# Two more projections ahead of the differential attention's loop, two cross-attention units in its last heads

## The reference, cut to what matters

```python
x = x + _L0_xattn_ref(_layernorm(x), ctx_2048, ...)   # stage X0
x = x + _L0_attn_ref(_layernorm(x), ...)              # stage A0
x = x + _L0_ffn_ref(_layernorm(x), ...)               # stage F0
x = x + _L1_xattn_ref(_layernorm(x), ctx_2048, ...)   # stage X1
x = x + _L1_attn_ref(_layernorm(x), ...)              # stage M1
x = x + _L1_ffn_ref(_layernorm(x), ...)               # stage F1
```

```python
q = (x @ Wq).reshape(b, s, h, 2, dh)       # dh = 64
k = (x @ Wk).reshape(b, s, h, 2, dh)
v = (x @ Wv).reshape(b, s, h, 2 * dh)
attn1 = softmax(einsum('bhsd,bhtd->bhst', q1, k1) * scale)
attn2 = softmax(einsum('bhsd,bhtd->bhst', q2, k2) * scale)
out = einsum('bhst,bhtd->bhsd', attn1 - lam * attn2, vh)
out = (out - mu) * rsqrt(var + EPS) * gw + gb          # per head
return out.reshape(b, s, -1) @ Wo
```

## Time and profile before

| | |
|---|---|
| three runs | 672.36 us median (667.4 to 675.68) |
| profiled execution, its own time | 668.17 us |
| its span | 666.4 us |
| PE busy | 639.1 us, 96% |
| DVE, ACT, POOL busy | 63%, 41%, 9% |
| granted PE clock, mean | 0.997 |

### The profile page before, as it was taken

One profiled execution on the slowest core, in us unless ns is written; L12 is line 12 of the kernel. 1 busy time (PEld: TensorE's weight loads), 2 busy tenths in 40 slices (PEclk: granted clock), 3 DMA queues, 4 the chain that ended last, 5 costly groups with the idle time before them and its releaser, 6 DMA issues.

```text
span 666.4 us, 21584 instructions
## 1 busy us (share of the span) xinstructions
PE 639.1 (96%) x9570; PEld 429.5 (64%) x9572; DVE 421.7 (63%) x982; ACT 274.4 (41%) x502; POOL 58.8 (9%) x130
## 2 busy tenths in 40 slices
PE   9999999999978999999999999999999999999876
PEld 4666667667565566666667565776777775466754
DVE  4544568587764765555564673554888965787487
ACT  2454445445442334333433754544554454011134
POOL 1020000000000100111111003000010101000000
PEclk9999999999998999999999999999999999999999
DMA  7243112117004500011002521111167200000001
GB/s 240 64 165 67 34 33 59 40 35 223 2 3 163 187 30 9 30 33 32 2 1 82 205 63 64 34 65 34 45 174 196 66 4 1 3 3 2 3 1 33
DMA packets 42365, 42.25 MB, mean 63 GB/s; under 512 B 15904, under 2 KB 33056, under 8 KB 42016
## 3 DMA queue, kind: packets, MB, share of 16 engines
q1 hardware_dynamic: 42272, 40.86, 19.8%
HBM read 40.33 MB, written 0.52 MB: 61 GB/s over the span
## 4 chain that ended last, share of the span: by engine, by line
PE 85%; DVE 10%; issue 2%; ACT 2%; POOL 0%; DVEq 0%; ACTq 0%; POOLq 0%
PE psum L379 16%; PE psum L387 16%; PE psum L1119 7%; PE psum L454 5%; PE psum L419 4%; PE psum L429 4%; PE psum L1170 4%; PE psum L1125 4%; PE psum L1860 2%; PE psum L404 2%; PE psum L1140 2%; PE psum L1839 2%; PE psum L1820 1%; PE psum L1154 1%; DVE arena L1956 1%
## 5 line engine op out<-in xcount | busy, mean ns | idle before, releaser
L379 PE MATMUL psum<-arena 128*128 128x512 f32 x256 | 121.6, 603 | 0.0
L387 PE MATMUL psum<-arena 128*128 128x256 f32 x512 | 121.5, 384 | 0.0
L387 PEld LDWEIGHTS psum<-arena 128*128 128x128 f32 x512 | 93.9, 190 | 21.6 <-issue 9.4
L379 PEld LDWEIGHTS psum<-arena 128*128 128x128 f32 x256 | 45.1, 191 | 43.7 <-issue 41.9
L674 ACT ACTIVATE arena<-arena 128x512 f32<-128x512 f32 x64 | 47.9, 804 | 35.5 <-DVE arena L798 35.5
L668 ACT ACTIVATE arena<-psum,arena 128x512 f32<-128x512 f32 x64 | 40.2, 687 | 31.0 <-DVE arena L785 30.9
L1119 PE MATMUL psum<-y_cols,arena 128*128 128x512 f32 x112 | 52.9, 605 | 0.0
L454 PEld LDWEIGHTS psum<-arena 128*17 128x17 f32 x4096 | 38.4, 96 | 20.7 <-issue 12.9
L798 DVE TENSOR_SCALAR arena<-psum 128x512 f32<-128x512 f32 x64 | 39.7, 682 | 17.9 <-PE psum L419 17.9
L1222 ACT ACTIVATE arena<-psum 128x512 f32<-128x512 f32 x48 | 28.2, 597 | 48.2 <-PE psum L1119 30.9
L785 DVE TENSOR_REDUCE arena<-psum 128x1 f32<-128x512 f32 x64 | 39.7, 684 | 12.8 <-PE psum L404 12.5
(11 more groups left out here) (248 smaller groups left out, 932.0 us busy)
## 6 DMA issues: line engine op xcount, KB each, us to landing
arena<-in_ctxT SPq DMA_DIRECT2D x32, 512.0 KB, 3.7
arena<-in_L_attn_Wv SPq DMA_DIRECT2D x1, 2048.0 KB, 8.4
arena<-in_L_attn_Wq SPq DMA_DIRECT2D x8, 256.0 KB, 2.9
arena<-in_L_attn_Wk SPq DMA_DIRECT2D x8, 256.0 KB, 3.5
arena<-in_L_attn_Wo SPq DMA_DIRECT2D x1, 2048.0 KB, 11.6
arena<-in_L_ffn_w_gating SPq DMA_DIRECT2D x1, 2048.0 KB, 7.9
arena<-in_L_attn_wo SPq DMA_DIRECT2D x2, 1024.0 KB, 6.3
arena<-in_wq_upT SPq DMA_DIRECT2D x2, 768.0 KB, 6.7
```

The lines of the kernel that those rows point to most:

```text
L379: last = nc.tensor.matmul(bank, wkv[:, c, i * P:(i + 1) * P], x[:, c, :], start=(c == 0), stop=(c == NC - 1))
L387: last = nc.tensor.matmul(bank[:, kk * D:(kk + 1) * D], x[:, c, k * P:(k + 1) * P], wkv[:, c, D:2 * D], start=(c == 0), stop=(c == NC - 1))
```

## The change

- `EARLY` goes from 4 to 6: the value projections of the first pair (g = 4 and 5) are made ahead too, in banks 2 and 3. Their tiles 0 and 1 go between `project_early(2, 4)` and `norm_turn` at the end of X0, tile 2 behind that turn, tile 3 between the tails in A0.
- The copies of the six go in the order 4, 0, 1, 5, 2, 3 (`ORDER`), the first of them inside X0, ahead of `norm_cols`. scores(0) waits for four copies instead of two, since it writes banks 2 and 3. The tail of g = 3 goes behind scores(0).
- `LEAD = 4` instead of 2: in each head the loop does the projections that are two further on. Head 0 loses one projection and gets another in its place. `load_pair(2)` waits for six projections instead of four.
- The last two projections that are so missing at the loop's end are replaced by units 0 and 1 of X1; units 2, 3 and 4 stand where 0, 1 and 2 stood, and only unit 5 stays behind the last out_rows.

The core of the diff:

```diff
             if after:
                 e.phases[A0].project_early(pe, 2, 4)
+                e.phases[A0].values_early(pe, 0, 2)
             next_turn(pe, NT - 1)
+            if after:
+                e.phases[A0].values_early(pe, 2, NT - 1)
...
             copy_out_cols(act, NT - 1)
+            if after:
+                e.phases[A0].copy_projected(act, 4)
             next_cols(act, NT - 1)
...
-            sp.wait_ge(s_proj, 6 * (p - 2) + 4)
+            sp.wait_ge(s_proj, 6 * (p - 2) + (6 if p == 2 else 4))
...
-    EARLY, HEAD = 4, (NT - 1) * P
+    EARLY, HEAD = 6, (NT - 1) * P
+    ORDER, LEAD = (4, 0, 1, 5, 2, 3), 4
...
+    def project_values(pe, p, t, bank):
+        for c in range(NC):
+            last = nc.tensor.matmul(bank[:, (t % 2) * 2 * DV:(t % 2 + 1) * 2 * DV], e.yT[:, c, t * P:(t + 1) * P],
+                                    wv[:, c, p * 2 * DV:(p + 1) * 2 * DV], start=(c == 0), stop=(c == NC - 1))
+        return last
+
+    def values_early(pe, *tiles):
+        pe.wait_ge(s_centre, 3 * PAIRS)
+        for t in range(*tiles):
+            last = project_values(pe, 0, t, home(4 + t // 2))
+        if t == 1:
+            last.then_inc(s_proj, 1)
...
-        pe.wait_ge(s_qkv, 6 * (h // 2) + 2 * u + 2)
+        pe.wait_ge(s_qkv, 6 * (h // 2) + 2 * u + 2 if h > 1 else (4, EARLY)[h])
...
-        for g in range(EARLY):
-            project_part(pe, g, slice(HEAD, ROWS)).then_inc(s_proj, 1)
+        tail = slice(HEAD, ROWS)
+        for g in (0, 1):
+            project_part(pe, g, tail).then_inc(s_proj, 1)
+        project_values(pe, 0, NT - 1, home(5)).then_inc(s_proj, 1)
+        project_part(pe, 2, tail).then_inc(s_proj, 1)
+        scores(pe, 0)
+        project_part(pe, 3, tail).then_inc(s_proj, 1)
         pe.wait_ge(s_zero, 2)
         pe.wait_ge(s_w, 16)
         for h in range(H):
-            g = 3 * h + 2
-            scores(pe, h)
+            g = 3 * h + LEAD
+            if h:
+                scores(pe, h)
             project(pe, g), project(pe, g + 1)
+            for u in units(1) if h == H - 1 else ():
+                e.phases[X1].unit_pe(pe, u)
...
             project(pe, g + 2)
+            if h == H - 2:
+                pe.wait_ge(s_qkv, 6 * PAIRS)
+                for u in units(0):
+                    e.phases[X1].unit_pe(pe, u)
             if h > 1:
                 out_rows(pe, h - 2)
-        pe.wait_ge(s_qkv, 6 * PAIRS)
-        for u in units(0):
+        for u in units(2):
             e.phases[X1].unit_pe(pe, u)
         turn(pe, H - 2)
         values(pe, H - 1)
-        for u in units(1):
+        for u in units(3):
             e.phases[X1].unit_pe(pe, u)
         out_rows(pe, H - 2)
         turn(pe, H - 1)
-        for u in units(2):
+        for u in units(4):
             e.phases[X1].unit_pe(pe, u)
         out_rows(pe, H - 1)
-        for u in units(3, 4, 5):
+        for u in units(5):
             e.phases[X1].unit_pe(pe, u)
```

More of the change, by code:

```diff
@@ L1088, in pool, with place @@
                 norm_power(nc, g, e, after, k)
-    EARLY, HEAD = 4, (NT - 1) * P
+    EARLY, HEAD = 6, (NT - 1) * P
+    ORDER, LEAD = (4, 0, 1, 5, 2, 3), 4
     def home(g):
-        return (B[0], B[1], B[4], B[5])[g] if g < EARLY else PROJ[g % 2]
+        return (B[0], B[1], B[4], B[5], B[2], B[3])[g] if g < EARLY else PROJ[g % 2]
+    def place(g):
+        return ORDER.index(g) + 1 if g < EARLY else g + 1
     def project_part(pe, g, cols):
@@ L1111, in project @@
             return
-        wait(pe, s_qkv, g - 1 if g >= EARLY + 2 else g - EARLY + 1)
+        wait(pe, s_qkv, place(g - 2 if g >= EARLY + 2 else g - EARLY))
         bank = PROJ[g % 2]
@@ L1120, in project @@
         else:
-            if g == 4:
-                pe.wait_ge(s_centre, 3 * PAIRS)
             for t in range(2 * j - 8, 2 * j - 6):
-                for c in range(NC):
-                    last = nc.tensor.matmul(bank[:, (t % 2) * 2 * DV:(t % 2 + 1) * 2 * DV], e.yT[:, c, t * P:(t + 1) * P],
-                                            wv[:, c, p * 2 * DV:(p + 1) * 2 * DV], start=(c == 0), stop=(c == NC - 1))
+                last = project_values(pe, p, t, bank)
         last.then_inc(s_proj, 1)
@@ L1214, in copy_projected @@
             return
-        act.wait_ge(s_proj, g + 1)
+        act.wait_ge(s_proj, place(g))
         if j < 4:
@@ L1231, in act @@
     def act(act):
-        for g in range(EARLY):
+        for g in ORDER[1:]:
             copy_projected(act, g)
@@ L1241, in act @@
                     copy_projected(act, i)
+            for u in units(1) if h == H - 1 else ():
+                e.phases[X1].unit_act(act, u)
             if h > 1:
                 copy_oT(act, h - 2)
-            copy_projected(act, g + 2)
+            if g + 2 >= EARLY:
+                copy_projected(act, g + 2)
+            for u in units(0) if h == H - 2 else ():
+                e.phases[X1].unit_act(act, u)
             if after:
@@ L1247, in act @@
         copy_oT(act, H - 2)
-        for u in units(0, 1):
+        for u in units(2, 3):
             e.phases[X1].unit_act(act, u)
         copy_oT(act, H - 1)
-        for u in units(2, 3, 4, 5):
+        for u in units(4, 5):
             e.phases[X1].unit_act(act, u)
@@ L1322, in attn @@
     return Named(pool=pool, pe=pe, act=act, dve=dve, load_early=load_early, load_pair=load_pair, load_out=load_out, project_early=project_early,
-                 centre_dve=centre_dve, small_dve=small_dve, small_act=small_act)
+                 values_early=values_early, copy_projected=copy_projected, centre_dve=centre_dve, small_dve=small_dve, small_act=small_act)
 E4M3_MIN = 2.0 ** -6
```

## The result

| | before | after |
|---|---|---|
| median of 20 runs each, side by side | 670.83 us | 668.36 us |
| lowest, highest | 667.4, 675.68 | 665.96, 670.27 |
| ratio, with its 95% interval | | 0.996 (0.9944 to 0.9975) |
| profiled execution, its own time | 668.17 us | 668.48 us |
| its span, mean granted clock | 666.4 us, 0.997 | 666.7 us, 0.997 |

The change is worth 1.7 to 3.8 us in this comparison. The forecast was 0.4 faster: the right class, too small a size. What has to be compared are stretches, and first it has to be found where they may begin.

The account below looks back on a forecast made before the run. PE, busy for 639.1 us, was taken as the bound. The terms +1.9 (scores(0)), +0.1 (exp), -3.46 (two units) and +1.1 (their cover) give -0.36 us; 0.4 off the median 672.36 is 672.0 us, range 666 to 676.

Parts of the forecast that it names:

- two chains: PE's order can't shorten scores(0) to scores(2), 10.96 us, or the last out_rows to F0's first matmul.
- the sum: All terms from A0's entry to F0 together: -0.36 us, with bounds of -1.0 to +0.4.
- scores(0) to scores(2): Start of A0: the chain over ACT and DVE stays 10.96 us, plus 0.1 for a later exp.
- the wait at scores(2): PE's wait for head 0's statistics in A0 stays, growing from 1.06 to about 1.3 us (1.1 to 1.5).
- scores(2) to scores(14): A0's loop: 36 projections either way, so again 12 x 9.00 us, 108 us.
- The second of F0's turns: At F0's start, PE was to wait for DVE's normed rows ahead of the turns, where it had not before.
- the hand-over: Last out_rows to F0's first matmul: two units fewer give 3.46 us, their lost cover costs 1.1.
- the last heads: Heads 14 and 15: unit 0 costs nothing; unit 1 saves 0.2 us, given back in turn(14)'s wait for DVE.
- The step that was mis-sized: scores(0): A0's entry: scores(0) starts 1.9 us later (+1.7 to +2.2), with a new PE wait of 0.45 for ACT's copy.
- rival 2: New waits at A0's or F0's entry lower PE's clock: 1.1 to 1.6 us slower, 673.5 to 674; chance 0.15.
- Rival 1: PE's filled waits around A0's entry and the last heads count in full: 2.2 us less, 670.2; chance 0.12.
- Rival 3: Context batch 3 lands 2 us or more later than said; PE waits some 0.5 us at unit 12; chance 0.05.

Follow-up runs that it names:

- e4: The whole change again, without an edit, beside the kernel before in a second comparison: 668.24 us, ratio 0.9971.
- e6: The kernel before, unedited, profiled once more: 672.6 us, mean granted clock 0.992.
- e10: The kernel before with five useless matmuls ahead of the turn, filling only the wait of 1.31 us: 669.68 us, ratio 1.0024.
- the entry alone: The kernel after with the units of cross attention back where they were before, on two chips: 669.86 us (ratio 0.9991) and 669.24 us (1.0028).
- e1: The kernel after with the units of cross attention back where they were before, first of two such runs: 669.86 us, ratio 0.9991.
- e2: The kernel before with unit 0 at the end of head 14, unit 1 in head 15, one unit behind the last out_rows: 670.05 us, ratio 0.9994.
- e11: The whole change with 16 useless small matmuls at the start and two wide ones instead of three: 670.9 us, ratio 1.0041 to the kernel before.
- e8: The whole change with 32 useless small matmuls at the program's start, 128 more PE instructions: 672.29 us, ratio 1.0044 to the kernel before.
- e12: The whole change with 48 useless small matmuls at the start and two wide ones instead of three: 667.69 us, ratio 0.9995 to the kernel before.

## Why the prediction was right, and where it was too small

**Right: the class and the mechanism.** Within 2% had 0.96, and the argument by two chains held. The range of 666 to 676 us says little for it, since it had to hold the spread of three runs. The stated 672.0 is 3.6 above what was measured: 1.5 because three runs gave 672.36 for before and twenty 670.83, 2.1 because the change was sized too small. By stretches the order gains 1.10, just outside the -1.0 to +0.4 of the sum. scores(0) to scores(2) was forecast at 11.06 and is 11.01; the wait at scores(2) was to be 1.1 to 1.5 and is 1.06; scores(2) to scores(14) is 108.05 for 108. The second of F0's turns waits for DVE (0.35), as said; the first doesn't. One reading was loose: in the chain of 10.96 us DVE and ACT don't both work without pause, ACT is idle for 3.01 us of it in one piece; they hand the head to each other, and it is the chain that has no gap.

**Right: the hand-over.** -3.46 for two units and +1.1 for their cover make -2.36; measured -2.33. A wait of 0.25 of unit 6 for the end of A0 on DVE was not foreseen; it lies inside what DVE's rows hold PE for anyway.

**Right: the last heads.** Unit 0 for a value projection in head 14 and unit 1 in head 15 cost nothing. The foreseen give-back is there in another shape: out_rows(13) waits 0.41 for ACT's copy, which has unit 1's copy ahead of it, and turn(14) waits 0.26, where it waited 0.35 before. The distance from scores(15) is 16.72 in both.

**The step that was mis-sized: scores(0).** Forecast +1.9, measured +1.13. The chain of steps was the right one, down to the new wait for ACT (0.24, forecast 0.45). But I added up durations. A group's duration in the profile runs to the end of its last matmul, and the next group starts while that one drains. `project_early` took 2.58 to the next start, not 2.74; the values 1.72, not 1.92; the turn 0.22, not 0.44; tile 3 0.86, not 0.96. These are 0.16 + 0.20 + 0.22 + 0.10 = 0.68 of the 0.77 missing. The pace could have been read from starts: I had used 1.72 for eight matmuls of the same size at the last heads. With these paces the sum would have been -1.04, and the measured -1.10 is what two profiles of the change give (159.53 and 159.54) and three of the moved ones.

**What the sum didn't hold.** The measured gain is 1.7 to 3.8 us (0.6 to 3.4 in e4's comparison), the order's 1.10. What is left has the sign opposite to rival 2: I gave 0.15 to a loss by the clock, and took 1.31 + 0.56 of waits as harmless because the one profile that I had went by without it. In e6 the same waits are followed by the lower level, for 1.6 us. So the prediction took the clock of before as settled by one profile, and left out that before itself has a lower-clock stretch more in many of its runs. How much of the gain comes from that stays open. The account that the change takes the place at the turn away would give 11 runs in 29 at 3.0 us each, 1.1 us, and with the order's 1.1 the 2.1 by which the medians of the first chip differ (670.34 - 668.24). But the means of the same runs give 0.38 for the clock, not 1.1, e10 and both runs of the entry alone gained nothing, and the place in M1 makes the same low clocks. What would test the account is the whole change against before on the third chip, where it gives 1.1 + 4/35 x 3.2 = 1.5 us; that wasn't run.

**Rival 1 fell.** The filled waits were not gained in full: of 2.2 us the order has 1.1, since the wait at scores(2) stands behind a chain that starts with scores(0), now later. The Trainium skill ("Perfetto Trace Analysis", Optimization Strategy) advises to find the gaps on the engine that one optimizes for, and what blocks it there; it doesn't say that a filled gap is gained, which was the rival's own step. That the measured total is near the rival's 2.2 is accident as far as the order goes. **Rival 3 fell**: unit 12 starts at 383.29 without a wait, with batch 3 landed 13.0 us after its issue at 369.2, that is at 382.2: 1.3 later than forecast, with 1.1 us of slack left.

## What to carry to other kernels

A wait that is filled counts up to the next chain that PE's order can't shorten: look for where that chain starts and whether the filling delays it; what is won early has to be spent on a place that would else stand empty, or it comes back as waits (e1, e2). Add up starts, not durations, of pipelined matmuls. When a change is worth under 1%, take stretches between two fixed instructions for the order, and the granted clock of every run for the rest: one profile of a kernel shows only one of its kinds of run. Instructions added to an engine as a test also move all that stands behind them in its stream; e10's twenty moved the cut in M1, so such a test changes two things at once.

## What the runs showed of the hardware that was not expected

**PE waits for its own instructions.** The long "issue" waits stand inside untouched runs of identical matmuls. The kernel after, PE's timeline ahead of A0:

```profile
195.49 1.69 PE L429 MATMUL psum<-ident,arena 128*128 128x128 f32 x14 [1.44 <-issue]
...
197.96 1.16 PE L454 MATMUL psum<-arena 128*17 128x32 f32 x111 [0.56 <-ACT y_cols L166]
201.31 0.32 PE L454 MATMUL psum<-arena 128*17 128x32 f32 x17 [2.20 <-issue]
```

The second wait cuts 128 equal matmuls behind the 111th. Between the two waits stand 14 of L429, the 2 of a turn (L158) and 111, so 127 matmuls, and as many weight loads: 254 instructions of PE. The page's part 3 has the loads of instructions:

```profile
q8 instruction: 76, 1.25, 0.8%
```

That is 76 packets of 1.25 MB together, 16.4 KB each. The Trainium skill ("Advanced Engine Details and Errata", ISA Cache) gives a cache line of 16 KB and 256 instructions; the trace agrees with both. What it costs is in PE's waits for "issue": 3.4 + 2.4 + 0.8 = 6.6 us in this profile, 2.2 the longest. That PE went through the 111 matmuls in 1.2 us and reached the next block before it was there is the reading that fits.

The traces bear it out further than I had seen. Number all of PE's instructions in a trace from its start, weight loads, matmuls and its sequencer's own (a few records may be missing). In the 14 profiles there are 73 "issue" waits of PE of 0.18 us or more, besides 14 short ones (0.29 to 0.33) ahead of values, and every one of the 73 ends 192 to 194 behind a multiple of 256, in the moved kernels too. The trace of after has 19,423 such instructions; they fill 76 blocks of 256, as many as q8 has packets. And in e10 the cut in M1 stands behind 21 of 32 equal matmuls, in before behind 31: ten matmuls and ten weight loads earlier, as many as e10 adds ahead of it.

Moved by 60 instructions (e11) and by 128 (e8), the cut is in another place:

```profile
196.16 1.11 PE L454 MATMUL psum<-arena 128*17 128x32 f32 x100
198.67 0.41 PE L454 MATMUL psum<-arena 128*17 128x32 f32 x28 [1.39 <-issue]
```

```profile
162.00 1.13 PE L454 MATMUL psum<-arena 128*17 128x32 f32 x106
165.00 0.36 PE L454 MATMUL psum<-arena 128*17 128x32 f32 x22 [1.87 <-issue]
```

e11's is 30 matmuls ahead of the old one at L429, as 60 instructions make it; the one that I had expected 30 ahead of the 111th did not appear, though the block ends there. e8's at 165 lies at the end of a block at which no unmoved kernel waited. So the rule that I had drawn, that the same wait moves along, was wrong: any end of a block may hold PE, and 4 to 7 of some 76 do in one run. Why some blocks come in time and others don't stays open.

**Such a wait can cost twice.** e8's windows behind its cut at 165:

```profile
164.00:168.00 4.00, 3.00 (x30) 2.44 (x31) 0.23 (x1) 0.28 (x1) 0.00 (x0) 0.75 0.43 148
168.00:172.00 4.00, 4.00 (x22) 3.06 (x21) 2.08 (x3) 1.19 (x2) 0.00 (x0) 0.83 0.00 0
```

Behind the wait of 1.87 us the clock falls, and from 200 to 204, where the uncut 128 matmuls are now (`201.06 1.31 PE L454`), e8 has 1.00, while e6 has 0.50 there. The stretches near 202 us stand behind such a wait too, and those in M1, and e11's one at 52 us (behind 3.13); the exceptions are those behind the turn. e12, moved by 188, has 1.1 us of these waits at L454 in all, 0.9 the longest, against 3.4 and 2.2 after, a mean clock of 1.000, and the shortest span of any profile, 664.7 us, though its start costs 2.2 to 2.7. Its median is at that of before on the third chip; whether it beats the whole change wasn't measured side by side. e11 shows that neither the clock nor one profile tells all: its runs at 0.996 or 0.997 average 670.03, before's on the same chip 667.61, and the one that was profiled, 668.42, was the second fastest of its ten.
